# Eight more halves of relation counts made in layer 2 and summed densely in layer 3 of a four-layer graph network

## The chip, the cores and the metric

The kernel runs on one core of one Trainium2 chip. The metric is device time in microseconds (us) for one execution. The core has five engines with queues of their own: PE (TensorE, matrix products), DVE (VectorE), ACT (ScalarE), POOL (GpSimd) and SP (SyncE). Here SP only issues plain DMAs and POOL in the two relational layers only issues gathers, each an indirect DMA that fetches 128 rows of a table.

## The reference, cut to what matters

There are 3125 nodes of 128 features and 100,000 edges, sorted by destination; each edge has one of 8 relations.

```python
# layers 0 and 1: two graph convolutions, then a residual and a layer norm
h   = leaky_relu(gcn_conv(x, src, dst, W1, b1))
x   = layernorm(x + gcn_conv(h, src, dst, W2, b2) * gate + bias)

# layers 2 and 3: two relational layers, then a residual and a layer norm
def rgcn_layer(x, W, SW, b):
    xt  = einsum('nd,rde->rne', x, W)        # a table row for each (relation, node)
    agg = segment_sum(xt[rel, src], dst, 3125)
    return relu(agg + x @ SW + b)
y   = rgcn_layer(rgcn_layer(x, w1, sl1, b1), w2, sl2, b2)
out = layernorm(x + y)
```

## The kernel before, in words

**Two ways to sum over edges.** In the relational layers a destination node gets its sum in one of two ways. *Dense*: the nodes are cut into halves of 32 (`HALF`). For each half a table of counts is made once: for each source node, how many edges it has to each of the 32 nodes by each of the 8 relations (25 source tiles of 128 nodes, 256 columns each, f16, 1.6 MB). Two halves form a pair; the features times the counts of a pair are summed over the 25 source tiles into 512 columns, and two pairs form a quad of 128 nodes, to which the relation weights are applied (`end_quad`, L1484 and L1487). *Sparse*: POOL gathers the table row of each edge, a chunk of 128 edges at a time (L853), and PE multiplies each chunk with a one-hot matrix of destinations (`add_message`, L1462). A chunk serves a window of 64 nodes, and one chunk follows the other at 4 nodes' distance, so that 8 nodes need 2 chunks.

**Who gets which.** `USED, MADE = 40, 48` (L57): layer 2 sums the nodes of 40 halves (1280) densely and gathers for the others; layer 3 sums those of 48 halves (1536) densely. All 48 tables are made in layer 2, beside its sums. Layer 2 has 469 gathers, layer 3 has 405.

**Making the counts.** A half is 8 strips of 4 nodes. For a strip DVE makes four one-hot tiles (`strip_hots`, L1861 twice and L1864 twice), PE multiplies them (`count_rstrip`, L1356, two products of 400 columns, two PSUM banks used by turns), and ACT copies the result into one of four buffers for halves (`turn_counts`, L984). SP stores a full half to memory (L722). 12 strips are counted ahead, beside the tables of layer 2's rows. `Made` works out the order of halves and buffers and deals the strips and the products of layer 2's sums (75 a pair: 25 tiles by 3 bf16 parts, L1427) out to 59 slots, one for each batch of 8 gathers. Two pairs (`STAY`) stay in their buffers and are neither stored nor loaded.

**Layer 3.** It has a slot for each batch of 8 gathers too (51). `spread_sums` deals the tiles of the dense sums out to all slots but the last three: 600 tiles, 25 of them ahead of slot 0, some 12 in a slot. For each tile ACT and DVE by turns widen the f16 counts to fp32 (L1038, L1998, up to 10 tiles ahead, 12 buffers) and PE does two products of 512 columns, with the high and the low part of the features (L1443, L1444). The messages of a slot's batch are set between its tiles. SP loads the counts of a pair (L712, two transfers) as soon as the pair before the previous one has been widened.

**What paces POOL.** In layer 3 POOL issues two gathers of batch n for each quarter of the tiles of slot n-2 that PE has done (a wait on `tile_summed`); in layer 2 the wait is on `rstrip_counted` in the same manner. Six batches of gathered rows have buffers.

```python
if layer == 3 and j % 2 == 0 and n >= AHEAD and sums3[n - AHEAD]:
    steps = steps_until[n - AHEAD + 1] - steps_until[n - AHEAD]
    pool.wait_ge(tile_summed, steps_until[n - AHEAD] + steps * (j // 2 + 1) // 4)
```

**Order on the engines.** Every engine runs a list that is written out ahead, slot by slot, and waits in order. In a slot of layer 2, DVE first copies and splits the tile of layer 3's table whose products PE made one slot earlier (`first_rows` L1985, `low_tile`), then makes the strips' one-hots two strips ahead (three buffers, `HOTS`), with the copy of a finished pair between them (`copy_sums2`, L1969), and then the one-hots of the next slot's batch (L1977). At the end of each node block or quad of layer 3 the result is turned, normalised and stored.

**Keys.** Before all that, with layer 0's counts (`pair_hots`, L1719), each group of 128 strips of two nodes has its relation keys made: the base from destination and source (`make_keys`, L1649), the relation gathered by POOL (L795) and added (`make_rel_keys`, L1670), the keys turned on PE (L1166) and copied by ACT (L900), three groups at a time. 48 halves need 6 groups.

Of the kernel before, what the change touches and what calls it, by code (L numbers as in the profile page):

```python
# [6 lines left out]
P = 128  # L7
# [29 lines left out]
GROUPS = -(-NP // (PAIR * P))  # L37
STRIPS = GROUPS * P
# [15 lines left out]
HSTRIPS = HALF // RSTRIP  # L54
RKEYS = R * TILES
RCELLS = PAIR * RKEYS
USED, MADE = 40, 48  # L57

LAST_BLOCK = 256
RGROUPS = -(-MADE * HALF // (PAIR * P))  # L60
RSTRIPS = RGROUPS * P
PER_CHUNK = 4
BACK, WIN = 32, 64
GATHERS, ONEHOTS, HOTS, RINGS = 6, 4, 3, 4
# [155 lines left out]
def gnn_kernel(nc, x, src, dst, rel, ctx_in, W1, b1, W2, b2, Wg, bg, Wb, w1, sl1, rb1, w2, sl2, rb2, out):  # L220
    f32, i32, f16, bf16 = mybir.dt.float32, mybir.dt.int32, mybir.dt.float16, mybir.dt.bfloat16
    f32r = mybir.dt.float32r
    ALU, ACT, AX = mybir.AluOpType, mybir.ActivationFunctionType, mybir.AxisListType
# [6 lines left out]
    with ExitStack() as stack:  # L230
# [10 lines left out]
        def sem(name):  # L241
# [17 lines left out]
        ident = sb("ident", [P, P])  # L259
# [5 lines left out]
        rel_cols = sb("rel_cols", [P, 2, RSTRIPS])  # L265
# [13 lines left out]
        xT = sb("xT", [P, NP])  # L279
        tin = sb("tin", [P, NP])  # L280
# [3 lines left out]
        dst_rows, src_rows, rel_rows, highs = (  # L284
            m.rearrange("p (g e) -> p g e", e=P) for m in (acc[:, 0:STRIPS], xT[:, 0:STRIPS], xT[:, STRIPS:STRIPS + RSTRIPS],
                                                           acc[:, STRIPS:STRIPS + 6 * P]))
        rel_bases = xT[:, STRIPS + RSTRIPS:STRIPS + 2 * RSTRIPS].rearrange("p (g e) -> p g e", e=P)
        hot_cols = edge_mem[:, 0:STRIPS].bitcast(f16).rearrange("p (a s) -> p a s", a=2)
        spare_rows = acc[:, STRIPS + 6 * P:STRIPS + 12 * P].rearrange("p (g e) -> p g e", e=P)

# [7 lines left out]
        def carve(at, n):  # L298
# [50 lines left out]
        ps = stack.enter_context(nc.psum_tensor("ps", [P, 8, BANK], f32))  # L349
# [11 lines left out]
        keys_ready, rel_keys_ready, keys_turned, cols_copied = (  # L361
            sem(n) for n in ("keys_ready", "rel_keys_ready", "keys_turned", "cols_copied"))
# [148 lines left out]

        key_events = [("strips", g) for g in range(GROUPS)] + [("relations", n) for n in range(RGROUPS // 3)]
        columns_until, n = [], 0
        for kind, g in key_events:
            n += 2 if kind == "strips" and g < RGROUPS else 1
# [369 lines left out]
        def _(act):  # L887
# [3 lines left out]
            def copy_columns(e):  # L891
                kind, n = key_events[e]
                act.wait_ge(keys_turned, e + 1)
                if kind == "strips":
                    keys = ps[:, KEY_BANK, 0:2 * P].rearrange("p (a s) -> p a s", a=2)
                    nc.scalar.activation(hot_cols[:, :, n * P:(n + 1) * P], keys, ACT.Copy).then_inc(cols_copied, 1)
                    if n < RGROUPS:
                        nc.scalar.activation(rel_cols[:, 0, n * P:(n + 1) * P], keys[:, 0, :], ACT.Copy).then_inc(cols_copied, 1)
                else:
                    nc.scalar.activation(rel_cols[:, 1, n * 3 * P:(n + 1) * 3 * P], ps[:, KEY_BANK, 0:3 * P], ACT.Copy).then_inc(cols_copied, 1)  # L900

            def evacuate_units(h):
                b, at = 2 * h // UNIT_BLOCK, 2 * h % UNIT_BLOCK * PAIR * CH
# [242 lines left out]
        def _(pe):  # L1146
# [8 lines left out]
            def turn_keys(e):  # L1155
                kind, n = key_events[e]
                if e:
                    pe.wait_ge(cols_copied, columns_until[e - 1])
                if kind == "strips":
                    pe.wait_ge(keys_ready, 1 + next(i for i, groups in enumerate(PREP_SETS) if n in groups))  # L1160
                    for a, rows in enumerate((src_rows, first_keys if n in PREP_SETS[0] else dst_rows)):
                        last = nc.tensor.transpose(ps[:, KEY_BANK, a * P:(a + 1) * P], rows[:, n, :], ident[:, :])
                else:
                    pe.wait_ge(rel_keys_ready, 1)
                    for a in range(3):
                        last = nc.tensor.transpose(ps[:, KEY_BANK, a * P:(a + 1) * P], rel_rows[:, 3 * n + a, :], ident[:, :])  # L1166
                last.then_inc(keys_turned, 1)

            pe.wait_ge(ident_ready, 1)
# [953 lines left out]
```

## Time and profile before

| | |
|---|---|
| time, median of 3 runs | 1634.54 us (1631.26 to 1634.96) |
| time of the profiled execution | 1633.26 us |
| span of the profiled execution, first to last instruction | 1631.4 us |
| mean granted clock of TensorE, 1 = 2.4 GHz | 0.962 |
| PE busy | 1434.2 us, 88% |
| POOL busy | 928.4 us, 57% |
| DVE busy | 907.0 us, 56% |
| ACT busy | 696.2 us, 43% |
| layer 2's slots, layer 3's slots | about 456 to 1082 us, about 1094 to 1622 us of the span |

Busy PE is not PE at its peak: a matmul's record reaches until its result is complete, and records overlap. What a product costs is the distance between the starts of two that follow each other without a gap. A row of a timeline that merges several instructions gives the start of the first.

### The profile page before, as it was taken

How to read it: one execution, taken by the hardware profiler on the slowest of the kernel's cores; microseconds unless marked ns; L12 is line 12 of the kernel's file. 1: busy time of each engine (PE TensorE's matmuls, PEld its weight loads, DVE VectorE, ACT ScalarE, POOL GpSimd, SP SyncE). 2: the span in 40 equal slices, each digit the busy share in tenths (PEclk: the TensorE clock that was granted, in tenths of full speed). 3: DMA queues.
4: the chain of work that ended last, by engine and by line, in shares of the span. 5: the costliest groups of instructions: out<-in, count | busy, mean ns of one | idle time of the engine just before them, and what ended most of it. 6: DMA issues, size and time to landing. Idle time of an engine off the chain costs nothing.

```text
span 1631.4 us, 24835 instructions
## 1 busy us (share of the span) xinstructions
PE 1434.2 (88%) x9144; PEld 986.7 (60%) x9144; DVE 907.0 (56%) x2665; ACT 696.2 (43%) x1024; POOL 928.4 (57%) x931
## 2 busy tenths in 40 slices
PE   1479989999879999999999999997888978889885
PEld 1364554444436656666666666666767867777775
DVE  8989992134756756657666765643333433334431
ACT  1465541011544645546455554553434444334430
POOL 6700000000067777767777777747777777777775
PEclk9999999999989999999999999998989998899997
DMA  4311340452455545646555554425655665555631
GB/s 135 122 82 82 132 176 37 161 203 101 180 183 173 212 158 199 213 172 215 185 192 209 187 186 177 132 91 213 215 215 214 215 219 199 187 182 214 220 126 48
DMA packets 67474, 275.82 MB, mean 169 GB/s; under 512 B 19988, under 2 KB 25854, under 8 KB 54676
## 3 DMA queue, kind: packets, MB, share of 16 engines
q1 hardware_dynamic: 37940, 213.87, 34.0%
q0 software_dynamic: 29408, 60.29, 13.3%
q8 instruction: 76, 1.25, 0.3%
q14 instruction: 50, 0.41, 0.1%
HBM read 153.70 MB, written 120.38 MB: 168 GB/s over the span
## 4 chain that ended last, share of the span: by engine, by line
PE 68%; DVE 14%; DMA 9%; issue 4%; POOL 4%; ACT 1%; POOLq 0%; DVEq 0%; ACTq 0%
PE ps L1427 20%; PE ps L1462 9%; DVE hot_mem L1719 9%; PE ps L1322 8%; PE ps L1443 8%; PE ps L1356 7%; PE ps L1444 6%; DMA node_id<-table_rel,edges 4%; DMA acc<-table_rel,edges 4%; PE ps L1501 3%; PE ps L1365 2%; POOL node_id L853 2%; PE ps L1487 2%; POOL acc L853 1%; DVE xn L1969 1%
## 5 line engine op out<-in xcount | busy, mean ns | idle before, releaser
L853 POOL DMA_INDIRECT node_id<-table_rel,edges x445 | 442.6, 995 | 499.5 <-DMA table_rel<-node_id 358.3
L853 POOL DMA_INDIRECT acc<-table_rel,edges x429 | 426.1, 993 | 155.0 <-issue 106.1
L1427 PE MATMUL ps<-blocks,raw 128*128 128x512 f16 x1500 | 440.9, 381 | 7.5 <-DVE xn L1969 6.7
L984 ACT ACTIVATE blocks<-ps 128x800 f16<-128x800 f32 x384 | 319.2, 837 | 230.4 <-PE ps L1356 228.7
L1462 PEld LDWEIGHTS ps<-raw,node_id 128*128 128x128 f32 x996 | 191.5, 200 | 113.3 <-issue 60.3
L1861 DVE TENSOR_SCALAR hot_mem<-cell_h,rel_cols 128x128 f16<-128x128 f16 x768 | 167.8, 273 | 160.4 <-PE ps L1356 158.2
L1462 PEld LDWEIGHTS ps<-raw,acc 128*128 128x128 f32 x962 | 179.9, 196 | 85.7 <-issue 37.5
L1864 DVE TENSOR_SCALAR hot_mem<-cell_h,rel_cols 128x400 f16<-128x400 f16 x768 | 226.2, 336 | 0.0
L1427 PEld LDWEIGHTS ps<-blocks,raw 128*128 128x128 bf16 x1500 | 160.1, 113 | 95.1 <-issue 15.0
L1462 PE MATMUL ps<-raw,node_id 128*128 128x64 f32 (+14 forms) x996 | 167.3, 255 | 55.8 <-DMA node_id<-table_rel,edges 55.8
L1356 PE MATMUL ps<-hot_mem 128*128 128x400 f16 x768 | 190.8, 334 | 3.9 <-DVE hot_mem L1864 2.6
L1462 PE MATMUL ps<-raw,acc 128*128 128x64 f32 (+13 forms) x962 | 157.4, 252 | 31.9 <-DMA acc<-table_rel,edges 31.9
L1719 DVE TENSOR_TENSOR hot_mem<-hot_mem,edges 128x2048 f16<-128x2048 f16 x200 | 164.0, 908 | 0.9 <-PE ps L1178 0.6
L1998 DVE CAST conv_hots<-blocks 128x512 fp32r<-128x512 f16 x150 | 65.2, 441 | 174.8 <-PE ps L1444 174.7
L1443 PE MATMUL ps<-conv_hots,high 128*128 128x512 f32 x300 | 147.5, 492 | 1.3 <-ACT conv_hots L1038 1.3
L1038 ACT ACTIVATE conv_hots<-blocks 128x512 fp32r<-128x512 f16 x150 | 92.6, 628 | 124.8 <-PE ps L1444 124.8
L1443 PE MATMUL ps<-conv_raw,high 128*128 128x512 f32 x300 | 138.3, 461 | 0.0
L1038 ACT ACTIVATE conv_raw<-blocks 128x512 fp32r<-128x512 f16 x150 | 93.1, 629 | 68.0 <-PE ps L1444 68.0
L1356 PEld LDWEIGHTS ps<-hot_mem 128*128 128x128 f16 x768 | 76.3, 107 | 74.9 <-issue 30.3
L1998 DVE CAST conv_raw<-blocks 128x512 fp32r<-128x512 f16 x150 | 68.2, 456 | 86.3 <-PE ps L1444 84.5
L1178 PE MATMUL ps<-hot_mem 128*128 128x50 f16 x1600 | 65.1, 195 | 51.4 <-DVE hot_mem L1719 49.9
L909 ACT ACTIVATE blocks<-ps 128x800 f16<-128x800 f32 x100 | 82.9, 837 | 61.5 <-PE ps L1178 61.3
(199 smaller groups left out, 1787.0 us busy)
## 6 DMA issues: line engine op xcount, KB each, us to landing
rcounts<-blocks SPq DMA_DIRECT2D x44, 1600.0 KB, 6.0
blocks<-rcounts SPq DMA_DIRECT2D x44, 1600.0 KB, 7.2
counts<-blocks SPq DMA_DIRECT2D x6, 3200.0 KB, 10.9
blocks<-counts SPq DMA_DIRECT2D x5, 3200.0 KB, 10.4
table_rel<-node_id SPq DMA_DIRECT2D x50, 256.0 KB, 2.1
table_rel<-xn SPq DMA_DIRECT2D x50, 256.0 KB, 2.4
node_id<-table_rel,edges POOLq DMA_INDIRECT x445
acc<-table_rel,edges POOLq DMA_INDIRECT x429
```

Source lines behind the costliest of these rows:

```text
L853: nc.gpsimd.indirect_dma_start(got[m % GATHERS][:, j, :], None, tables_rel[layer - 2], bass.IndirectOffsetOnAxis(ap=row_i[:, first + j:fir ...
L984: nc.scalar.activation(to.rearrange("p t (b m) -> p t b m", b=2), ps[:, strip_bank(k):strip_bank(k) + 2, 0:RCELLS].rearrange("p b (m t) -> ...
L1038: nc.scalar.activation(wide_tile(i).rearrange("p (h n) -> p h n", h=2), narrow_tile(i), ACT.Copy).then_inc(act_wide, 1)
L1322: nc.tensor.matmul(total, part, buffer_of(i)[:, t * n:(t + 1) * n], start=first, stop=False)
L1356: last = nc.tensor.matmul(ps[:, strip_bank(k) + c, 0:RCELLS], rlow_hot[:, k % HOTS, c, :], rcell_hot[:, k % HOTS, c, :], start=True, stop= ...
L1427: last = nc.tensor.matmul(ps[:, SUM_BANK, 0:2 * HCOLS], parts[:, c, t, :], half_pairs[u % 2][:, :, t * HCOLS:(t + 1) * HCOLS], start=(k == ...
L1443: nc.tensor.matmul(ps[:, u % 2, 0:2 * HCOLS], high3(t), wide_tile(i), start=(k == 0), stop=False)
L1462: last = nc.tensor.matmul(ps[:, GATHER_BANK, a - start_:b - start_], got[m % GATHERS][:, j, :], nodehot[:, m % ONEHOTS, j, a - base:b - ba ...
L1719: last = nc.vector.tensor_tensor(hot[:, u, :, :, :], each_h[:, 0:n, :].unsqueeze(1).to_broadcast([P, CH, n, 2]), keys.unsqueeze(2).to_broa ...
L1861: nc.vector.tensor_scalar(rlow_hot[:, u, c, :], cell_h[:, 0:P], rel_cols[:, 0, first + c:first + c + 1], 0.0, ALU.subtract, ALU.is_equal)
L1864: last = nc.vector.tensor_scalar(rcell_hot[:, u, c, :], cell_h[:, :], rel_cols[:, 1, first + c:first + c + 1], 0.0, ALU.subtract, ALU.is_e ...
L1998: nc.vector.tensor_copy(wide_tile(i).rearrange("p (h n) -> p h n", h=2), narrow_tile(i)).then_inc(dve_wide, 1)
```

## The change

56 halves are made in layer 2 in place of 48, and layer 3 sums all 56 (1792 nodes) densely. Layer 2 still uses 40. What follows from the constants: 64 more strips; 28 pairs in layer 3 in place of 24 (700 tiles in place of 600, 14 quads in place of 12); 341 gathers in layer 3 in place of 405, so 43 slots in place of 51, with 17 tiles in a slot in place of 12; 386 messages in place of 450; 52 halves stored and 52 loaded in place of 44 each. Layer 2 keeps its 59 slots and 469 gathers, with 6 to 8 strips in most slots in place of 5 to 8; 41 slots have 8, before 10 did; of the 23 slots in which DVE copies a tile of the table, 17 have 8, before 3 did. Seven groups of relation keys in place of 6 are turned in steps of four and three in place of three and three, and their bases lie in `tin` in place of `xT`, where seven groups would not fit.

```diff
--- before.py
+++ after.py
@@ -54,11 +54,12 @@
 HSTRIPS = HALF // RSTRIP
 RKEYS = R * TILES
 RCELLS = PAIR * RKEYS
-USED, MADE = 40, 48
+USED, MADE = 40, 56
 
 LAST_BLOCK = 256
 RGROUPS = -(-MADE * HALF // (PAIR * P))
 RSTRIPS = RGROUPS * P
+REL_TURNS = [range(a, min(a + 4, RGROUPS)) for a in range(0, RGROUPS, 4)]
 PER_CHUNK = 4
 BACK, WIN = 32, 64
 GATHERS, ONEHOTS, HOTS, RINGS = 6, 4, 3, 4
@@ -284,7 +285,7 @@
         dst_rows, src_rows, rel_rows, highs = (
             m.rearrange("p (g e) -> p g e", e=P) for m in (acc[:, 0:STRIPS], xT[:, 0:STRIPS], xT[:, STRIPS:STRIPS + RSTRIPS],
                                                            acc[:, STRIPS:STRIPS + 6 * P]))
-        rel_bases = xT[:, STRIPS + RSTRIPS:STRIPS + 2 * RSTRIPS].rearrange("p (g e) -> p g e", e=P)
+        rel_bases = tin[:, 0:RSTRIPS].rearrange("p (g e) -> p g e", e=P)
         hot_cols = edge_mem[:, 0:STRIPS].bitcast(f16).rearrange("p (a s) -> p a s", a=2)
         spare_rows = acc[:, STRIPS + 6 * P:STRIPS + 12 * P].rearrange("p (g e) -> p g e", e=P)
 
@@ -511,7 +512,7 @@
 
 
 
-        key_events = [("strips", g) for g in range(GROUPS)] + [("relations", n) for n in range(RGROUPS // 3)]
+        key_events = [("strips", g) for g in range(GROUPS)] + [("relations", n) for n in range(len(REL_TURNS))]
         columns_until, n = [], 0
         for kind, g in key_events:
             n += 2 if kind == "strips" and g < RGROUPS else 1
@@ -897,7 +898,8 @@
                     if n < RGROUPS:
                         nc.scalar.activation(rel_cols[:, 0, n * P:(n + 1) * P], keys[:, 0, :], ACT.Copy).then_inc(cols_copied, 1)
                 else:
-                    nc.scalar.activation(rel_cols[:, 1, n * 3 * P:(n + 1) * 3 * P], ps[:, KEY_BANK, 0:3 * P], ACT.Copy).then_inc(cols_copied, 1)
+                    own = REL_TURNS[n]
+                    nc.scalar.activation(rel_cols[:, 1, own[0] * P:(own[-1] + 1) * P], ps[:, KEY_BANK, 0:len(own) * P], ACT.Copy).then_inc(cols_copied, 1)
 
             def evacuate_units(h):
                 b, at = 2 * h // UNIT_BLOCK, 2 * h % UNIT_BLOCK * PAIR * CH
@@ -1162,8 +1164,8 @@
                         last = nc.tensor.transpose(ps[:, KEY_BANK, a * P:(a + 1) * P], rows[:, n, :], ident[:, :])
                 else:
                     pe.wait_ge(rel_keys_ready, 1)
-                    for a in range(3):
-                        last = nc.tensor.transpose(ps[:, KEY_BANK, a * P:(a + 1) * P], rel_rows[:, 3 * n + a, :], ident[:, :])
+                    for a, g in enumerate(REL_TURNS[n]):
+                        last = nc.tensor.transpose(ps[:, KEY_BANK, a * P:(a + 1) * P], rel_rows[:, g, :], ident[:, :])
                 last.then_inc(keys_turned, 1)
 
             pe.wait_ge(ident_ready, 1)
```

## Rows read from the trace of the kernel before

**Rows 1.** Windows by stage: busy us (instructions) of each engine, granted clock, DMA share, GB/s.

```profile
456.00:1082.00 626.00, 603.74 (x3550) 387.62 (x3551) 398.91 (x1584) 327.80 (x425) 466.94 (x468) 0.99 0.52 181
...
1111.50:1600.80 489.30, 423.75 (x2228) 360.11 (x2229) 174.04 (x423) 198.13 (x330) 374.06 (x379) 0.92 0.55 195
```

**Rows 2.** Waits of PE in layer 2, 456 to 1082: us in total, times, longest.

```profile
PE ps L1462 <- DMA node_id<-table_rel,edges: 7.8, 1, 7.8
PE ps L1427 <- DVE xn L1969: 6.7, 12, 1.2
...
PE ps L1356 <- DVE hot_mem L1864: 1.0, 3, 0.4
```

**Rows 3.** Waits of PE in layer 3, 1111.5 to 1600.8.

```profile
PE ps L1462 <- DMA node_id<-table_rel,edges: 41.2, 11, 6.6
PE ps L1462 <- DMA acc<-table_rel,edges: 26.4, 10, 4.5
```

**Rows 4.** Timeline of PE in a stretch of layer 2: start us, us, what.

```profile
863.26 0.50 PE L1356 MATMUL ps<-hot_mem 128*128 128x400 f16 x2
863.60 0.81 PE L1427 MATMUL ps<-blocks,raw 128*128 128x512 f16 x3
864.25 0.33 PE L1462 MATMUL ps<-raw,node_id 128*128 128x64 f32 x2
864.41 0.59 PE L1427 MATMUL ps<-blocks,raw 128*128 128x512 f16 x2
```

**Rows 5.** Timeline of PE in a stretch of layer 3 without a gap.

```profile
1158.92 0.33 PE L1462 MATMUL ps<-raw,acc 128*128 128x64 f32 x2
...
1160.07 0.33 PE L1462 MATMUL ps<-raw,acc 128*128 128x64 f32 x2
...
1168.10 0.33 PE L1462 MATMUL ps<-raw,acc 128*128 128x64 f32 x2
1168.27 0.44 PE L1484 MATMUL ps<-tin,ws 128*128 128x128 f32 x2
...
1170.25 0.47 PE L1443 MATMUL ps<-conv_hots,high 128*128 128x512 f32 x1
```

**Rows 6.** Window of a stretch of layer 2 in which slots have 8 strips.

```profile
920.00:950.00 30.00, 29.46 (x180) 18.97 (x179) 24.66 (x102) 19.99 (x24) 22.93 (x24) 1.00 0.59 215
```

**Rows 7.** Timeline of DVE in layer 2: copy of a pair, then one-hots, three strips apart.

```profile
548.18 1.03 DVE L1969 COPY xn<-ps 128x512 f32<-128x512 f32 x1 [0.36 <-PE ps L1427]
...
550.52 0.41 DVE L1861 TENSOR_SCALAR hot_mem<-cell_h,rel_cols 128x128 f16<-128x128 f16 x2
...
553.01 0.42 DVE L1861 TENSOR_SCALAR hot_mem<-cell_h,rel_cols 128x128 f16<-128x128 f16 x2
```

**Rows 8.** Chain that ended last: layer 3's first gather, the eighth, its landing.

```profile
1095.79 0.94 POOL acc L853
...
1104.73 6.79 DMA acc<-table_rel,edges
1111.65 0.56 PE ps L1462 x2
...
1278.81 3.62 DMA acc<-table_rel,edges
```

**Rows 9.** Timeline: the first gather after the last tile, the last gather, the last messages.

```profile
1601.91 0.94 POOL L853 DMA_INDIRECT acc<-table_rel,edges  x1 [0.30 <-issue]
...
1618.14 0.94 POOL L853 DMA_INDIRECT node_id<-table_rel,edges  x1 [0.30 <-issue]
...
1621.41 2.37 PE L1462 MATMUL ps<-raw,node_id 128*128 128x64 f32 x10 [3.81 <-DMA node_id<-table_rel,edges]
```

**Rows 10.** Loads of halves in layer 3: us from issue to landing.

```profile
DMA to landing us min/median/max: 6.8/7.2/8.8
```

**Rows 11.** DMA share of the stretch in which a pair was loaded, 1123 to 1133.

```profile
1123.00:1133.00 10.00, 5.92 (x33) 4.83 (x31) 3.19 (x7) 4.00 (x6) 7.56 (x9) 0.89 0.93 374
```

**Rows 12.** Relation keys of six groups: duration min/median/max.

```profile
L1670 DVE SCALAR_TENSOR_TENSOR xT<-xT x1: 954/954/954, 89.9 to 89.9; 128x768 f32<-128x768 int32 x1
```

## The prediction

> **What bounds the kernel now.** I read the busy times by stage first, then PE's waits in the two relational layers, then stretches of the timeline for the price of each product. In layer 2 PE is busy 603.7 of 626 us at a granted clock of 0.99, while POOL is busy 467 [rows 1]; PE waits there once for a gather, 7.8 us at the start, and else in small change [rows 2]. Layer 2 is PE's. In layer 3 PE is busy 423.8 of 489.3 us at 0.92 [rows 1], and it waits for gathered rows 21 times, 67.6 us in all [rows 3]. POOL starts 405 gathers between 1095.79 and 1618.14, the first and the last start: 1.29 us each [rows 8, 9]. Started without a gate they lie 1.25 us apart, as in the stretch after the last tile: 13 steps in 16.2 us [rows 9]. 405 x 1.25 = 506 of these 522 us, so layer 3 is POOL's, and PE's waits are what it has left over. The change takes gathers from POOL in layer 3 and gives PE work in both layers. So the question is what PE needs in each.
>
> **Keys.** One group more: the relation keys on DVE take 0.95 us for six groups [rows 12], so 0.16 more; the base, a transpose, a copy and one more relation gather (POOL is idle there afterwards) are of the same size or hidden. Moving the bases to `tin` costs nothing: `tin` is first written by `scale_x`, four pairs later on the same engine. I take 0.5 us, between 0 and 2.
>
> **Layer 2: 64 more strips.** A strip's two products take 0.34 us on PE (863.26 to 863.60), a product of the dense sum 0.22 and a message 0.16 [rows 4]. PE is the bound, so all of 64 x 0.34 = 21.8 us lies on the path. Beside it: ACT has 64 more copies on an engine busy 328 of 626 us [rows 1], hidden. DVE's one-hots take 0.83 us a strip when nothing gates them (550.52 to 553.01, three strips) [rows 7], so 53 us more on 399 [rows 1], or 452 of some 649: hidden on average. But DVE works in order, 41 slots now have 8 strips and 17 of these also a table tile to copy; a copy of a pair, 1.03 us [rows 7], stands ahead of one-hots, which are made only two strips ahead. In the stretch of such slots that the trace has, DVE was busy 24.7 of 30 us and PE 29.5 [rows 6], and waits of PE for one-hots come to 1.0 us in all of layer 2 [rows 2]. I take 1 us, and 0 to 20 as bounds (half a microsecond in each of 41 slots). SP's 8 more stores of 1.6 MB: a load of that size lands in 7.2 us [rows 10], the DMA engines' share in layer 2 is 0.52 [rows 1], and a buffer comes back only after the next half's 8 strips: hidden; without that cover a store would cost its 7 us. Gathers in layer 2 stay 469; they are paced by strips, and a slot grows from 10.6 to 11 us against POOL's 10.0, so POOL gets slack. Layer 2: +22.8 us.
>
> In the same stretch POOL issued 24 gathers in 30 us, 1.25 us apart, beside a DVE busy for 82% [rows 6]. The Trainium skill, "SBUF — State Buffer", section "Who interferes with whom", says that a DVE operation in a two-port mode, which these one-hots and the casts of layer 3 can be, locks GpSimd out for its whole length, so that descriptors of POOL's DMAs can't be written. By that rule the 53 us of new one-hots would be POOL's loss. The trace does not agree: at 82% of DVE a pace of 1.25 us could not stand.
>
> **Layer 3 on POOL.** 64 gathers fewer: 341 x 1.25 = 426 us, 80 less.
>
> **Layer 3 on PE.** In the stretch without a gap, 1158.92 to 1160.07 holds two tiles and one message (1.15 us), and 1158.92 to 1168.10 holds 15 tiles and 10 messages (9.18 us) [rows 5]. So a tile costs 0.464 and a message 0.222 us, and a quad 1.98 (1168.27 to 1170.25). Counted from the first message at 1111.65 [rows 8], when 27 tiles are done, to the last tile (21 messages and one quad lie behind it):
> - before: 573 tiles 265.9, 429 messages 95.2, 11 quads 21.8, block starts and turns some 7.5 (allowance): 390.4 us, against 489 measured, ending at 1600.8;
> - after: 673 tiles 312.3, 365 messages 81.0, 13 quads 25.7, 7.5: 426.5 us.
>
> A slot of 17 tiles and 8 messages is 9.7 us, 10.4 on average with quads and block starts; POOL's slot is 10.0. So PE becomes the bound, by little. Will it run gapless? The last two gathers of batch n are released by the end of slot n-2, take 2.5 us to issue and 6.8 to land [rows 8], 9.3 us; PE needs them after slot n-1 and three tiles, 10.4 + 1.4 = 11.8 later. 2.5 us are left. That is the order of layer 2 (10.6 against 10.0 and the same gates), where PE's idle time, without the first wait, is 14.5 of 626 us, 2.3% [rows 1, 2]. I take 10 us for this, and 3 for half-clock time and for slots 0 to 3, where POOL's batches land just as PE comes. The last tile then ends at 1111.65 + 426.5 + 13 = 1551.2: 49.6 us earlier.
>
> **The end.** After the last tile 14 gathers were left (1601.91 to 1618.14), then the landing, ten products and the last norm, 30.6 us in all [rows 9]. If PE sets the pace, 7 are left, those released by the last tile and the last batch of 5, or 8.8 us less; if POOL lags, nothing is won. I take 6.6.
>
> **Loads.** A pair of halves takes about 11 us to land (7.2 each, overlapping) [rows 10], at a DMA share of 0.93 [rows 11]. It is sent for when the pair before the previous one is widened and is needed 25 tiles later: 21.7 us before, 25/17 x 10.4 = 15.3 after. 4 us are left, and 10 widened tiles beyond that. Hidden. But gathers landed in 3.6 us where no load ran and in 6.8 beside one [rows 8]; now a load runs 7 us in 10, so the late landing becomes the rule. I have priced it so.
>
> **The sum.** 0.5 + 22.8 - 49.6 - 6.6 = -32.9 us. The profiled execution took 1633.3 us (span 1631.4), so 1600.4; the median of the runs shown is 1.3 above it: 1602 us. Its own range: 1588 (no allowance in layer 3, 8.8 at the end) to 1612 (twice the allowances). A measurement of this kernel can tell some 0.3% (5 us) from no change.
>
> **Rivals.**
> - *A third of the stalls stays.* Layer 3 loses 489 - 390 = 99 us to waits and half clock, 2.06 us a slot. If a third of it stays in 40 slots: 27 us in place of 13, and the end gains 3.6 less. 1620. For it: PE's and POOL's slots differ by only 0.4 us, and the clock falls with each wait of some 3 us.
> - *Half of it stays*: 41 us, the end gains 2 in place of 6.6: 1634, no change.
> - *Lock step, slower.* The gates and the landing, not POOL's number of gathers, make the stalls, and all 2.06 us a slot stay: 82 in place of 13, nothing gained at the end: 1602 + 69 + 7 = 1678. It decides when a landing takes over 9.3 us from issue (6.8 + 2.5), since each slot then ends late and releases its gathers late. Against it: layer 2 has the same gates, nearly the same slot, and hardly a wait [rows 2].
> - *DVE bounds layer 2.* Half a microsecond in 41 slots: 1621. Against it: [rows 6].
> - *The port.* Were POOL's 1.25 us partly DVE's lock, the 53 us would lengthen layer 2 in place of 22: 1633. The pace beside a busy DVE speaks against it [rows 6].
>
> **Chances.** Forecast 0.66; a third of the stalls 0.14; DVE 0.06; half the stalls 0.05; lock step 0.07; port 0.02. Faster by over 0.3%: 0.66 + 0.14 + 0.06 = 0.86. Same: 0.05 + 0.02 = 0.07. Slower: 0.07. The range reaches from 1588 to the third of the stalls and DVE's case with 3 us on top, 1624, and leaves out the rest.
>
> **What the profile would show.** Layer 2 some 23 us longer with PE busy as before and waits on one-hots under 3 us; 448 strips. Layer 3's last tile 50 us earlier on its own clock, that is near 1574; PE's waits for gathers under 20 us there, in place of 67.6; the granted clock at 0.97 or more; gathers 1.3 to 1.35 us apart, now with POOL waiting for tiles; and 7 or 8 gathers behind the last tile. A clock still near 0.92 and a wait in every second slot would show the stalls kept; a wait of the casts for loads would show that loads are not hidden; PE waits on L1864 of 10 us or more would show DVE's case.

## The result and the profile after

| | before | after |
|---|---|---|
| median of the runs, us | 1633.79 (4 runs) | 1579.34 (1579.26 to 1579.51, 4 runs) |
| ratio, 95% interval | | 0.967 (0.965 to 0.968) |
| span of the profiled execution, us | 1631.4 | 1577.7 |
| mean granted clock | 0.962 | 0.988 |
| PE's first to last product of layer 2's sums, us | 623.9 | 640.3 |
| start of the first to start of the last tile of layer 3, us | 506.8 | 444.6 |
| start of the last tile to the end of the span, us | 30.9 | 22.7 |

54 us faster. The forecast was faster by 32 and a range down to 1588: the direction held, the size did not. Two lines are added, one near the top and one at L901, so that line numbers of after are one higher up to there and two higher behind: L1429 is L1427 of before, L1358 is L1356, L1445 and L1446 are L1443 and L1444, L1464 is L1462, L854 is L853, L2000 is L1998.

The page of the changed kernel, its busy line and the clock in 40 slices:

```profile
PE 1452.0 (92%) x9381; PEld 999.4 (63%) x9381; DVE 978.1 (62%) x2967; ACT 785.2 (50%) x1147; POOL 866.8 (55%) x868
...
PEclk9999999999989999999999999999999999999998
```

The windows by stage, as in [rows 1], here cut where the changed kernel's stages lie (busy us and instructions of each engine, granted clock, DMA share, GB/s). The second begins at the first message of layer 3, the third after the last tile:

```profile
456.00:1099.00 643.00, 623.82 (x3681) 399.34 (x3681) 451.67 (x1843) 381.48 (x490) 468.54 (x468) 0.99 0.56 197
...
1128.40:1555.60 427.20, 425.89 (x2337) 365.43 (x2338) 191.28 (x464) 233.43 (x387) 317.78 (x322) 0.99 0.67 245
1555.60:1577.70 22.10, 9.23 (x67) 8.32 (x65) 5.46 (x19) 2.56 (x6) 7.64 (x8) 0.71 0.15 40
```

In layer 3 PE is busy 425.9 of 427.2 us, where before it was busy 423.8 of 489.3. So it now bounds layer 3, with only one gap, of 1.0 us, after the first message. The waits of PE (engine, line, whom it waited for: us in total, times, longest), first in layer 2, where they answer to [rows 2]:

```profile
PE ps L1429 <- DVE xn L1971: 8.6, 16, 1.2
PE ps L1464 <- DMA node_id<-table_rel,edges: 7.5, 1, 7.5
...
PE ps L1358 <- DVE hot_mem L1866: 0.6, 2, 0.3
```

Layer 2 of before had one wait more for a gather, which neither [rows 2] nor the prediction shows. It ends at 573.1 us; in the changed kernel only the wait at the start (7.5 us) is left:

```profile
PE ps L1462 <- DMA acc<-table_rel,edges: 2.3, 1, 2.3
```

In layer 3 of the changed kernel, from the first message to the last tile, the waits answer to [rows 3]:

```profile
PE ps L1464 <- DMA acc<-table_rel,edges: 4.6, 1, 4.6
PE ps L1457 <- ACT tin L1063: 1.0, 1, 1.0
```

21 waits for gathered rows of 67.6 us together have become one of 4.6 us, the one at the first message. POOL's gathers of layer 3 (duration in ns, first and last start, and what POOL's idle time before them ended on):

```profile
L854 POOL DMA_INDIRECT acc<-table_rel,edges x173: 938/944/1360, 1112.5 to 1564.4; - x173
L854 POOL DMA_INDIRECT node_id<-table_rel,edges x168: 940/944/2639, 1123.1 to 1533.9; - x168
...
  PE ps L1446: 43.0, 103
```

341 gathers in 451.9 us are 1.33 us each, and 43.0 us of POOL's idle time end on a tile of PE (L1446), that is on the gates, in place of 24.7 us before (81 times, on L1444). The loads of halves, which the prediction hid, took to landing:

```profile
DMA to landing us min/median/max: 6.9/7.2/8.2
```

### The profile page after: what moved, and what is told of

It is laid out like the page before. It is cut to its first block, busy times and chain, and to the rows that moved or that the text cites. A ratio compares the mean times of both kernels' runs of the same rounds, so it can differ in the third digit from the quotient of the medians.

```text
span 1577.7 us, 25737 instructions
## 1 busy us (share of the span) xinstructions
PE 1452.0 (92%) x9381; PEld 999.4 (63%) x9381; DVE 978.1 (62%) x2967; ACT 785.2 (50%) x1147; POOL 866.8 (55%) x868
## 4 chain that ended last, share of the span: by engine, by line
PE 79%; DVE 15%; issue 2%; POOL 2%; DMA 1%; ACT 1%; POOLq 0%; DVEq 0%; ACTq 0%
PE ps L1429 20%; PE ps L1445 11%; PE ps L1446 10%; PE ps L1464 9%; DVE hot_mem L1721 9%; PE ps L1358 9%; PE ps L1324 8%; PE ps L1503 3%; PE ps L1489 3%; PE ps L1367 3%; DVE xn L1971 1%; DMA acc<-table_rel,edges 1%; POOL acc L854 1%; POOL acc L796 1%; POOL node_id L854 0%
## 5 line engine op out<-in xcount | busy, mean ns | idle before, releaser
L854 POOL DMA_INDIRECT node_id<-table_rel,edges x408 | 409.6, 1004 | 502.1 <-DMA table_rel<-node_id 358.7
L854 POOL DMA_INDIRECT acc<-table_rel,edges x402 | 397.9, 990 | 160.1 <-issue 92.4
L986 ACT ACTIVATE blocks<-ps 128x800 f16<-128x800 f32 x448 | 372.6, 836 | 209.7 <-PE ps L1358 204.9
L1429 PE MATMUL ps<-blocks,raw 128*128 128x512 f16 x1500 | 440.7, 380 | 8.6 <-DVE xn L1971 8.6
L1863 DVE TENSOR_SCALAR hot_mem<-cell_h,rel_cols 128x128 f16<-128x128 f16 x896 | 193.7, 272 | 132.9 <-PE ps L1358 127.8
L1866 DVE TENSOR_SCALAR hot_mem<-cell_h,rel_cols 128x400 f16<-128x400 f16 x896 | 260.4, 332 | 0.0
L1358 PE MATMUL ps<-hot_mem 128*128 128x400 f16 x896 | 222.5, 333 | 3.6 <-DVE hot_mem L1866 2.3
L1429 PEld LDWEIGHTS ps<-blocks,raw 128*128 128x128 bf16 x1500 | 157.6, 111 | 102.7 <-issue 16.3
L1464 PEld LDWEIGHTS ps<-raw,node_id 128*128 128x128 f32 x906 | 169.2, 190 | 55.6 <-issue 9.1
L1464 PEld LDWEIGHTS ps<-raw,acc 128*128 128x128 f32 x924 | 168.7, 192 | 56.2 <-issue 13.2
L1464 PE MATMUL ps<-raw,acc 128*128 128x64 f32 (+10 forms) x924 | 146.6, 247 | 10.7 <-DMA acc<-table_rel,edges 10.7
L1445 PE MATMUL ps<-conv_hots,high 128*128 128x512 f32 x352 | 154.0, 438 | 1.3 <-ACT conv_hots L1040 1.3
L1464 PE MATMUL ps<-raw,node_id 128*128 128x64 f32 (+10 forms) x906 | 146.3, 244 | 7.5 <-DMA node_id<-table_rel,edges 7.5
L1445 PE MATMUL ps<-conv_raw,high 128*128 128x512 f32 x348 | 152.4, 438 | 0.1
L1358 PEld LDWEIGHTS ps<-hot_mem 128*128 128x128 f16 x896 | 89.3, 109 | 80.1 <-issue 31.2
L1040 ACT ACTIVATE conv_hots<-blocks 128x512 fp32r<-128x512 f16 x176 | 108.2, 630 | 60.4 <-PE ps L1446 60.1
L2000 DVE CAST conv_hots<-blocks 128x512 fp32r<-128x512 f16 x176 | 78.8, 458 | 87.7 <-PE ps L1446 86.7
L2000 DVE CAST conv_raw<-blocks 128x512 fp32r<-128x512 f16 x174 | 76.4, 449 | 81.7 <-PE ps L1446 80.7
L911 ACT ACTIVATE blocks<-ps 128x800 f16<-128x800 f32 x100 | 82.8, 838 | 61.2 <-PE ps L1180 61.0
```

The lines of the kernel that those rows point to most:

```text
L854: nc.gpsimd.indirect_dma_start(got[m % GATHERS][:, j, :], None, tables_rel[layer - 2], bass.IndirectOffsetOnAxis(ap=row_i[:, first + j:fir ...
L986: nc.scalar.activation(to.rearrange("p t (b m) -> p t b m", b=2), ps[:, strip_bank(k):strip_bank(k) + 2, 0:RCELLS].rearrange("p b (m t) -> ...
L1040: nc.scalar.activation(wide_tile(i).rearrange("p (h n) -> p h n", h=2), narrow_tile(i), ACT.Copy).then_inc(act_wide, 1)
L1358: last = nc.tensor.matmul(ps[:, strip_bank(k) + c, 0:RCELLS], rlow_hot[:, k % HOTS, c, :], rcell_hot[:, k % HOTS, c, :], start=True, stop= ...
L1429: last = nc.tensor.matmul(ps[:, SUM_BANK, 0:2 * HCOLS], parts[:, c, t, :], half_pairs[u % 2][:, :, t * HCOLS:(t + 1) * HCOLS], start=(k == ...
L1445: nc.tensor.matmul(ps[:, u % 2, 0:2 * HCOLS], high3(t), wide_tile(i), start=(k == 0), stop=False)
```

## The experiments

Each kernel was timed in turns with the kernel before on the same chip; the ratio is to that, with its 95% interval.

**The keys alone.** All of the changed code, with the old number of halves.

```diff
-USED, MADE = 40, 56
+USED, MADE = 40, 48
```

> 48 halves as before, with the new code for the relation keys: turned in steps of four and two groups in place of three and three, bases in the other memory. My theory (the whole change lies in the two relational layers): 1634 us, within 3. Rival (the keys' part carries some of the 54 us gained, or costs some): 5 us or more away from 1634.

1634.6 us, ratio 1.000 (0.999 to 1.002). The turning of the keys in other steps and their other memory cost nothing and bring nothing that can be measured. This kernel has six groups of keys, not seven; the seventh is made before layer 2, whose first product of sums starts at 456.6 us in the changed kernel and at 456.3 before, so it costs nothing that shows either.

**52 and 60 halves.**

```diff
-USED, MADE = 40, 56
+USED, MADE = 40, 52
```

> 52 halves made and dense in layer 3. My theory (layer 3 lasts as long as the longer of POOL's and PE's work): POOL needs 373 x 1.25 = 466 us there, PE some 409, so layer 3 is still POOL's. At before's 1.29 us a gather it is 32 x 1.29 = 41 us shorter than before, layer 2 is 32 x 0.34 = 11 us longer less up to 5 for a wait that goes away: 1599 to 1604 us, with PE waiting for gathers 20 us or more in layer 3. Rival (gain in proportion to the halves, no change of bound): half way, 1607 us.

1603.5 us, ratio 0.981 (0.979 to 0.983), within what was expected. Waits of PE in its layer 3:

```profile
PE ps L1464 <- DMA acc<-table_rel,edges: 22.9, 8, 4.5
PE ps L1464 <- DMA node_id<-table_rel,edges: 11.5, 5, 3.8
```

13 waits for gathers, 34.4 us (4.5 of them at the first message): at 52 halves layer 3 is still POOL's. The time is also only 3.5 us from the rival's 1607; it is the waits that decide between the two.

```diff
-USED, MADE = 40, 56
+USED, MADE = 40, 60
...
-        stats = sb("stats", [P, TILES, 6])
+        stats = sb_over("stats", [P, TILES, 6], f32, "wgate")
```

> 60 halves made and dense in layer 3. My theory (at 56 halves PE already bounds layer 3): 50 tiles more x 0.464 = 23, 32 messages fewer x 0.222 = 7, a quad 2, and 32 strips x 0.34 = 11 in layer 2: 29 us more than the changed kernel, 1608 us. Rival (POOL's gathers still bound at 56 halves, and 27 us go with every 4 halves): 1552 us.

1601.1 us, ratio 0.980 (0.978 to 0.982): 22 us slower than at 56, and not 29. The direction and the bound are as expected. The window of its layer 3:

```profile
1138.00:1577.00 439.00, 437.87 (x2354) 373.90 (x2354) 195.90 (x484) 251.03 (x414) 280.55 (x290) 1.00 0.68 249
```

And the waits of PE in its layer 2:

```profile
PE ps L1464 <- DMA node_id<-table_rel,edges: 6.4, 1, 6.4
PE ps L1429 <- DVE xn L1971: 5.3, 11, 0.5
```

PE is busy 437.9 of 439 us of layer 3, as good as gapless again. My sum for it was too high for reasons that can be read off: 60 halves leave three node blocks for the gathers in place of four, so one edge between blocks less, where 15 chunks are multiplied twice (47 messages fewer than at 56 halves, not 32; 3.3 us), and in layer 2 the waits for the copy of a pair (L1429 behind DVE) shrank from 8.6 to 5.3 us; and in layer 3 the mean clock is 1.00 in place of 0.99. 56 is the lowest of the three.

**The halves made, but not used.** 56 halves in layer 2; layer 3 sums 48 and gathers for the rest. The numbers of the halves are exchanged so that the two that stay in their buffers are 46 and 47.

```diff
-USED, MADE = 40, 56
+USED, MADE, DENSE3 = 40, 56, 48
...
-        gathers = {2: Gathers(USED * HALF), 3: Gathers(MADE * HALF)}
+        gathers = {2: Gathers(USED * HALF), 3: Gathers(DENSE3 * HALF)}
...
-        STEPS3 = TILES * (MADE // 2)
+        STEPS3 = TILES * (DENSE3 // 2)
```

> 56 halves are made in layer 2, but layer 3 sums 48 densely and gathers for the rest as before; the result is whole. My theory: layer 2 grows by the 16.7 us seen in the changed kernel (21.8 for 64 strips, less 5 for the wait for a gather at 577 us that goes away in longer slots): 1651 us. Rival (strips are cheaper than 0.34 us and the wait at 577 has nothing to do with it): that wait is seen again. Rival (the number of halves in layer 2 is paid again in layer 3's loads or end): over 1656 us.

1649.5 us, ratio 1.010 (1.008 to 1.012), 16.1 above the kernel before beside it. Layer 2's part is 16 to 17 us, as in the changed kernel, and not the 22.8 of my sum. Why it is less shows in one stretch, 570 to 600 us. Before, with 48 halves:

```profile
570.00:600.00 30.00, 27.06 (x154) 17.28 (x153) 17.40 (x69) 13.87 (x18) 22.69 (x25) 0.94 0.44 146
```

The same stretch with the keys alone (48 halves):

```profile
570.00:600.00 30.00, 27.07 (x156) 17.42 (x155) 17.57 (x68) 13.78 (x19) 22.70 (x24) 0.94 0.47 162
```

With layer 3 alone (48 halves, below):

```profile
570.00:600.00 30.00, 27.06 (x155) 17.30 (x153) 17.31 (x69) 13.74 (x19) 22.69 (x25) 0.94 0.45 146
```

With 52 halves:

```profile
570.00:600.00 30.00, 29.34 (x178) 19.10 (x177) 20.42 (x82) 16.32 (x21) 22.69 (x25) 1.00 0.50 172
```

The changed kernel, with 56:

```profile
570.00:600.00 30.00, 29.62 (x182) 19.26 (x180) 21.02 (x84) 17.25 (x22) 22.69 (x24) 1.00 0.56 195
```

And 56 halves made but not used:

```profile
570.00:600.00 30.00, 29.63 (x180) 19.25 (x179) 20.06 (x81) 17.13 (x23) 22.68 (x25) 1.00 0.59 213
```

With 48 halves PE is busy 27.1 of 30 us at a clock of 0.94, in all three kernels; with 52 or more 29.3 to 29.6 at 1.00. POOL starts 24 or 25 gathers in each: it runs at its full pace of 1.25 us in all six. With 48 halves most slots up to there have 5 or 6 strips and PE needs less than POOL's 10 us for one, so it catches up with POOL and waits for a gather, from 570.8 to 573.1; with 8 strips in most of them it does not. With 52 halves the slots are longer only in part, and two short waits (1.0 and 1.3 us) end at 626 and 637 us instead. The 64 strips cost the 64 x 0.34 = 21.8 us of the sum: PE is busy 623.8 us in place of 603.7 [rows 1], 20.1 more, and 0.06 of 30 us of clock, or 1.8, are no longer in that. What comes back is these 1.8 and idle time: 22.3 us before and 643.0 - 623.8 = 19.2 after, 3.1 less. 2.3 of this is the wait for the gather. The other 0.8 is what is left of small changes both ways: the waits for the copy of a pair grew from 6.7 to 8.6 us, others fell by some 2.7.

**Layer 3 alone.** 48 halves made, layer 3 sums 28 pairs; the four pairs more are loaded from other nodes' counts.

```diff
-USED, MADE = 40, 56
+USED, MADE, DENSE3 = 40, 48, 56
...
-PAIR_ORDER3 = [*STAY, *(w - 1 for w in STAY)]
+STAY3 = (DENSE3 // 2 - 1, USED // 2 - 1)
+PAIR_ORDER3 = [*STAY3, *(w - 1 for w in STAY3)]
...
-rcounts_dram[2 * PAIR_ORDER3[p] + h, :, :]
+rcounts_dram[2 * {23: 0, 24: 1, 25: 2, 26: 3}.get(PAIR_ORDER3[p], PAIR_ORDER3[p]) + h, :, :]
```

> 48 halves are made as before, layer 3 sums 56 densely; the counts of the eight more halves (nodes 1472 to 1791) are those of other nodes, loaded from memory a second time. My theory (the layers' shares add up): 62 us less between layer 3's first and last tile and 8 less behind it, as in the changed kernel, with layer 2 as before: 1563 us. Rival (layer 3's gain needs the longer layer 2, say by POOL or DMA work that is over by then): 1570 us or more.

1561.9 us, ratio 0.955 (0.953 to 0.957). The kernel before beside it took 1636.9, so 75.0 less; against the 1633.8 of before elsewhere, 71.9. The layers' parts add up to within 1.3 to 4.4 us: +16.1 and -72 to -75 against -54.5 of both.

**Fewer gathers, no more tiles.** The kernel before, with layer 3's gathers from node 1792 on.

```diff
-        gathers = {2: Gathers(USED * HALF), 3: Gathers(MADE * HALF)}
+        gathers = {2: Gathers(USED * HALF), 3: Gathers(56 * HALF)}
```

> The kernel before (48 halves) with layer 3's gathers from node 1792 on in place of 1536: the messages of nodes 1536 to 1791 are left out in layer 3, and their output. My theory (layer 3 of before is POOL's work alone): 64 gathers fewer at 1.29 us, 82 us less, 1551 us, that is more than the 71 us that layer 3 gave in the changed kernel, where PE became the bound; PE still waits for gathers, since it has 600 tiles only. Rival (layer 3's time comes from PE's and POOL's waits for each other, whatever the number of gathers per slot): the same 10.0 us a slot as before, but 2.06 us a slot of waits and half-clock time stay and PE's share is unchanged: less than 71 us are won.

That run, and the two of the end in the same batch (below), fell on a chip on which the kernel before took 1853 us (1826 to 1874), and ACT and DVE waited up to 11 us at a time for something that the profile puts outside the core; 1758.3 us, ratio 0.955 (0.947 to 0.964), tells nothing about some microseconds. So it was run again:

> Again the kernel before with layer 3's gathers from node 1792 on in place of 1536 (the messages of nodes 1536 to 1791, and their output, left out), since the times of its first run and of the kernel before beside it scattered by over 2%. My theory, as before: 64 x 1.29 = 82 us less, 1551 us, more than the 71 us of the changed kernel's layer 3. Rival: less than 71 us.

1557.9 us, ratio 0.952 (0.950 to 0.955), 76.2 less than the kernel before beside it. POOL's gathers in its layer 3:

```profile
L853 POOL DMA_INDIRECT acc<-table_rel,edges x173: 939/947/1360, 1099.3 to 1544.4; - x173
L853 POOL DMA_INDIRECT node_id<-table_rel,edges x168: 941/946/3128, 1109.9 to 1517.4; - x168
```

And PE's waits from the first message to the last tile:

```profile
PE ps L1462 <- DMA node_id<-table_rel,edges: 19.5, 8, 3.4
PE ps L1462 <- DMA acc<-table_rel,edges: 10.5, 6, 4.5
```

341 gathers from 1099.3 to 1544.4 are 1.31 us each, near the 1.29 of before, and PE, with only 600 tiles, still waits 14 times. So fewer gathers shorten layer 3, and by more than the changed kernel's 71, though by 6 to 7 us less than the 82 expected. The messages of these 64 gathers are left out with them, but they are only 64 x 0.222 = 14 us of PE's work and could not give 76. That before's layer 3 was bound by its gathers, and not by PE's products, is shown.

**One PSUM bank for layer 3's sums,** as layer 2 has it.

```diff
-                        if u >= 2:
-                            pe.wait_ge(half_copied, PAIRS2 + u - 1)
+                        if u:
+                            pe.wait_ge(half_copied, PAIRS2 + u)
...
-                    nc.tensor.matmul(ps[:, u % 2, 0:2 * HCOLS], high3(t), wide_tile(i), start=(k == 0), stop=False)
+                    nc.tensor.matmul(ps[:, 0, 0:2 * HCOLS], high3(t), wide_tile(i), start=(k == 0), stop=False)
```

> The changed kernel with layer 3's sums in one PSUM bank in place of two by turns, as layer 2 has it: the next pair's first product waits until ACT has copied the last one's sum. My theory (PE's small change of waits in layer 2 comes from that one bank and from a late gather, and layer 3 has neither, so it runs gapless): the copy takes 1.1 us and a semaphore each way, 27 times some 1.4 us, 38 us more: 1617 us. Rival (the wait is filled by work already queued): 1580 us.

1622.1 us (1615.1 to 1627.5), ratio 0.991 (0.987 to 0.994), 43 us above the changed kernel; the profile is of a run of 1626.8. Its waits in layer 3:

```profile
PE ps L1445 <- ACT raw L1048: 30.4, 26, 3.3
PE ps L1464 <- DMA acc<-table_rel,edges: 3.9, 2, 3.1
```

26 waits for ACT's copy of a pair's sum, 30.4 us. Layer 2 has this wait in small (8.6 us in 16 waits, above), layer 3 with its two banks has none.

**POOL's gates later.**

```diff
-pool.wait_ge(tile_summed, steps_until[n - AHEAD] + steps * (j // 2 + 1) // 4)
+pool.wait_ge(tile_summed, min(steps_until[n - AHEAD] + steps * (j // 2 + 1) // 4 + 8, STEPS3))
```

> The changed kernel with POOL's gates in layer 3 eight tiles (nearly half a slot, 4.6 us) later. My theory (a batch's last gathers are 9.3 us from release to landing and have 2.5 us to spare): first message to first message becomes 3 us of tiles to the release and 9.3 for the gather, 12.3 us in place of 10.4, some 38 times: 72 us and some half-clock time on top, 1650 to 1675 us. Rival (POOL runs far enough ahead, so the gates have much more than 2.5 us to spare): 1579 to 1590 us.

1620.1 us (1616.1 to 1626.4), ratio 0.991 (0.987 to 0.994). 41 us slower than the changed kernel, so the gates have only a few microseconds to spare; but not the 72 expected, so it is more than my 2.5. PE's waits for gathers in its layer 3:

```profile
PE ps L1464 <- DMA node_id<-table_rel,edges: 14.5, 11, 2.7
PE ps L1464 <- DMA acc<-table_rel,edges: 14.4, 7, 4.5
```

These are 18 waits, 28.9 us, and 4.5 of it is the wait at the first message, which the changed kernel has too (4.6). So 17 of 40 slots have a new wait, 24.4 us together: a gate 4.6 us later costs 0.6 us a slot. That puts the spare time at 4.0 us or more in the mean over the slots, an estimate from this one shift; in the slots that wait it was less than 4.6, in the others more. The rest of the 41 us is mostly time at half clock (mean clock 0.980 in place of 0.988, some 13 us), and a longer end. I had priced every landing at 6.8 us; some land sooner, as the one in 3.62 us [rows 8].

**36 halves used in layer 2.** An attempt to shorten layer 2, where PE is the bound in the changed kernel.

```diff
-USED, MADE = 40, 56
+USED, MADE = 36, 56
```

> 56 halves made, but 36 in place of 40 summed densely in layer 2, 32 gathers more there. PE has 150 products x 0.217 less and 32 messages x 0.16 more: 27 us less. POOL has 501 gathers x 1.25 = 626 us in place of 586, against a layer 2 of 643. My theory (each layer lasts as long as the longer of the two): layer 2 becomes POOL's, 626 and some waits: 1565 to 1580 us. Rival (POOL never bounds layer 2): 1552 us. Rival (waits and half clock as in layer 3 of before): 1590 us or more.

1589.0 us, ratio 0.971 (0.970 to 0.973): 10 us slower than the changed kernel, out of my range and nearest to the last of the three cases (1590 us or more). POOL's gathers of its layer 2:

```profile
L854 POOL DMA_INDIRECT node_id<-table_rel,edges x259: 941/947/1772, 456.2 to 1104.1; - x130
L854 POOL DMA_INDIRECT acc<-table_rel,edges x240: 940/947/1700, 487.7 to 1080.3; - x120
```

And PE's waits there:

```profile
PE ps L1464 <- DMA acc<-table_rel,edges: 17.5, 9, 6.1
PE ps L1464 <- DMA node_id<-table_rel,edges: 10.4, 4, 8.0
```

499 of the 501 gathers, from 456.2 to 1104.1, are 1.30 us each, and PE waits 13 times, 27.9 us. So this layer 2 runs at about the 1.29 of before's layer 3, not at the 1.25 that I had taken here.

**The end.** Layer 3's tiles dealt out to all slots but the last two, or but the last one, in place of three.

```diff
-        a, b = (n + n * (pairs - 1) * min(t, slots - 3) // (slots - 3) for t in (s, s + 1))
+        a, b = (n + n * (pairs - 1) * min(t, slots - 2) // (slots - 2) for t in (s, s + 1))
```

> The changed kernel with layer 3's tiles dealt out to all slots but the last two in place of the last three. My theory (behind the last tile the path is POOL's: gathers released by it or unissued, 1.25 us each, a landing, ten products and the last norm): the last batch of 5 is released before the last tile, so 5 gathers fewer, some 6 us, and 8 messages move ahead of it: 1573 us, within 2. Rival (the end is PE's or the norms' work): 1579 us.

> The changed kernel with layer 3's tiles dealt out to all slots but the last one. My theory: all gathers are issued before the last tile's slot ends, but the last quad and its norm now stand behind the last tile and the last messages: 1570 to 1574 us. Rival (the last quad's chain costs more than the gathers saved): 1576 us or more.

Both fell on the chip that scattered: 1782.3 and 1790.5 us, ratios 0.966 (0.958 to 0.975) and 0.971 (0.962 to 0.981), inconclusive. The first was run again with the changed kernel beside it:

> Again the changed kernel with layer 3's tiles dealt out to all slots but the last two, for the same reason. My theory: 5 gathers fewer behind the last tile, 6 us: 1573 us, within 2. Rival (the end is PE's or the norms' work): 1579 us.

> The changed kernel once more, beside the two others on one chip, as the base for the few microseconds at the end: 1579 us, within 2.

1577.5 us (1577.4 to 1578.9, five runs), ratio 0.965 (0.964 to 0.967), and 1580.1 us (1579.5 to 1581.9, five runs), ratio 0.967 (0.965 to 0.969). The first is 2.6 us faster; the runs of the two do not overlap. It is the fastest whole kernel of this study, but by less than half of what was expected. Windows of its end, up to its last tile and behind it:

```profile
1556.00:1563.30 7.30, 7.30 (x40) 6.18 (x39) 1.86 (x6) 0.63 (x1) 5.47 (x7) 1.00 0.21 56
1563.30:1577.00 13.70, 5.78 (x50) 5.35 (x48) 3.32 (x13) 2.37 (x5) 0.56 (x1) 0.86 0.10 26
```

13.7 us are left behind the last tile in place of some 22, but the tile itself ends 7 us later than in the changed kernel beside it (1563.3 against 1556.5). Some 3 us of this are messages that stood behind it and now stand ahead. The rest is mostly waits: PE's waits from the first message to the last tile are these,

```profile
PE ps L1464 <- DMA acc<-table_rel,edges: 5.1, 2, 4.2
PE ps L1464 <- DMA node_id<-table_rel,edges: 2.3, 2, 1.5
```

and beside the one at the first message (4.2 us) they hold three of 3.2 us together, where the changed kernel has none. That is about the 3.4 us by which the gain fell short of the 6 expected. The same tiles in one slot more are fewer in a slot (16.5 in place of 16.9 in the mean), which brings PE nearer to POOL; that this is why the waits are back is argued, not tested.

## Why the prediction was wrong

**Right.** What bounds which layer, and that the bound moves from POOL to PE. The sum of PE's products in layer 3, within 1%: 426.5 us worked out from two stretches of the timeline [rows 5], 426.6 measured from the first message (1128.6) to the last product of the last tile (1555.2), the point that was 1600.8 before. That the two agree to 0.1 us is luck. The measured time also holds a gap of 1.0 us and a stretch at half clock right behind the first message, which costs some 3 us:

```profile
1128.40:1134.70 6.30, 6.08 (x18) 5.09 (x19) 1.01 (x3) 1.26 (x2) 4.78 (x6) 0.51 0.23 57
1134.70:1555.60 420.90, 419.81 (x2321) 360.34 (x2320) 190.27 (x462) 232.17 (x385) 313.00 (x317) 1.00 0.68 248
```

So the products themselves took about 422.5, and the sum, with its 7.5 us of allowance for block starts, was 4 too high. The price of a strip, 0.34 us, and DVE and ACT beside it: DVE is busy 451.7 of 643 us and PE waits 0.6 us for one-hots. The loads stayed hidden (7.2 us again). The keys cost nothing that can be measured; I had taken 0.5. One reading was loose: the landing of 3.62 us [rows 8], put down as one "where no load ran", fell into the end of a load, at a DMA share of 0.69 against 0.95 for the landing of 6.79.

**The step that failed: the allowance in layer 3.** "I take 10 us for this, and 3 for half-clock time" is what the prediction set on the 426.5, with the 2.3% of idle time that layer 2 has beside its first wait. The last tile came 426.6 us after the first message and not 439.5: 12.9 of the 21 us of error lie here. The 3 us for half clock came. Of the 10 only a gap of 1.0 us came, which is 9 us of error; the other 4 are the sum that was too high. Layer 2's idle time was read as what two engines of nearly equal pace cost each other. Most of it is something else, in the trace of before already. Of its 14.5 us, 6.7 are waits for the copy of a pair [rows 2], which come with the one bank of layer 2's sums; 2.6 stand ahead of a quad's products (L1484) with no wait that the profile shows; and only 2.3, the wait that ends at 573.1 us, are for a gather. Layer 3 has two banks, and with one bank it lost 43 us. And here PE, 0.4 us a slot slower than POOL, had no wait for it behind the first message: six batches have buffers, and the spare time is nearer to 4 us than to the 2.5 that I had counted.

**The step mis-sized in layer 2.** "All of 64 x 0.34 = 21.8 us lies on the path", and 1 more for DVE and 0.5 for the keys: 23.3, measured 16.4 to 17 (16.7 at the first tile of layer 3, 1110.4 against 1093.7). The products are the right price. What the sum lacked is that longer slots also take away a wait of before: the gathers that bounded layer 3 bounded layer 2 for a moment too, up to 573.1 us. "PE waits there once for a gather" was a misreading: there were two such waits, the second of 2.3 us with a stretch at half clock behind it, and they make 4.1 of the some 5 us that came back. The windows of six kernels with 40 halves used show it, by the number of halves made alone. The first message came at 1128.6 and not at 1111.65 + 23.3: 6.3 us of the error.

**The end.** 6.6 us were taken, 8.1 came (22.5 from 1555.2 to the end of the span, in place of 30.6). In the trace of the changed kernel (start, duration), the last gathers after the last tile, and the last messages:

```profile
1555.22 0.39 PE L1446 MATMUL ps<-conv_hots,low 128*128 128x512 f32 x1
1555.22 0.42 PEld L1464 LDWEIGHTS ps<-raw,node_id 128*128 128x128 f32 x2
1555.32 0.95 POOL L854 DMA_INDIRECT acc<-table_rel,edges  x1 [0.30 <-issue]
...
1564.43 0.94 POOL L854 DMA_INDIRECT acc<-table_rel,edges  x1 [0.30 <-issue]
...
1567.79 2.36 PE L1464 MATMUL ps<-raw,acc 128*128 128x64 f32 x10 [5.15 <-DMA acc<-table_rel,edges]
```

8 gathers start after 1555.22, in place of 14: 7.5 us less, where I had counted 7 and 8.8. Of the 2.2 us that I had held back for a POOL that lags, 1.5 were not needed.

12.9, 6.3 and 1.5 are 20.7 us, which is the error: the span expected was 1598.5, the measured one 1577.7.

**The rivals.** A third or half of the stalls, or all of them, did not stay: one wait of 4.6 us and a granted clock of 0.99 in layer 3 against 0.92. Waits on the gates are a real danger here, though: with the gates 4.6 us later 24 us of waits are back and the kernel takes 41 us more, though not the 72 expected there. DVE did not bound layer 2. The port: POOL's gathers in layer 2 keep their duration, with a median of 945 ns (944 and 945 before), while DVE's work there grew from 399 to 452 us:

```profile
L854 POOL DMA_INDIRECT node_id<-table_rel,edges x240: 938/945/1681, 454.4 to 1072.5; - x120
L854 POOL DMA_INDIRECT acc<-table_rel,edges x229: 938/945/1807, 485.7 to 1095.2; - x115
```

So the rule of the Trainium skill ("SBUF — State Buffer", "Who interferes with whom") that a two-port operation of DVE stops GpSimd's descriptors does not show in these one-hots. No run here shows in which mode they ran.

**The range.** Its low end, 1588 (1602 less 13 and less 2.2 is 1587), left out the allowances of layer 3 but held layer 2's 22.8 fixed, with no lower bound beside 0 to 20 more. A change of slots that takes a wait away is a gain that the rows allowed: PE's 22.3 us of idle time in layer 2 [rows 1] were the room for it. With layer 2 as long as predicted the kernel would have taken 1579.3 + 6.3 = 1585.6 us, still a little below that end, by the sum of products that was 4 too high.

## What to carry to other kernels

Where one engine feeds another, price the next bound as the plain sum of its own instructions, each from a stretch without a gap; add idle time only with a cause that the new order also has, not as a percentage of a neighbouring stage. Before adding it, ask of every wait of the old trace whether the change also removes it, in the stages that are only made longer too. In this kernel a layer that the feeding engine bounded ran 3 to 5% over that engine's unhindered pace (1.29 to 1.31 against 1.25 us a gather, three times), and one that the fed engine bounded ran within 1% of its sum. Of the three splits tried the best is the one in which the fed engine is just the slower one. The margin is thin: with the same tiles dealt out to one slot more, 3 us of waits were back.

## What was not expected of the hardware

With one bank for layer 3's sums, the granted clock was once at half for 17 us (1521.9 to 1539.0) though no wait of PE just before it was long. Three windows of that kernel:

```profile
1500.00:1530.00 30.00, 26.96 (x132) 22.89 (x132) 10.56 (x25) 13.74 (x23) 17.14 (x18) 0.87 0.62 234
1530.00:1550.00 20.00, 18.87 (x87) 16.06 (x86) 7.17 (x24) 7.28 (x13) 9.62 (x9) 0.78 0.47 169
1550.00:1570.00 20.00, 18.59 (x105) 15.80 (x104) 8.61 (x22) 9.97 (x17) 13.13 (x15) 1.00 0.67 242
```

From 1530 to 1550 PE is busy 18.9 of 20 us and the mean clock is 0.78; just before the fall it had two waits, of 1.04 and 1.03 us, that end at 1520.0 and 1522.3. From 1550 to 1570 it is busy 18.6 of 20 us at 1.00. Both levels (1.2 and 2.4 GHz) were so granted at nearly the same busy share, though a busy PE does less at the lower one (87 matmuls against 105). Single waits of about 1 us, some 16 us apart, stand all along this layer and left the clock at full elsewhere. It need not happen: of the six runs of this kernel three took 1627 us at a mean clock of 0.980 and three 1615 to 1618 us at 0.986 to 0.988. That this stretch is the whole difference is not shown, since the profile is of one of the three of 1627 us and none was taken of the others. In the changed kernel layer 3 ran at full clock but for the stretch behind the first message.

Whether a gather lands in 3 or 7 us seems to go with the loads beside it (3.62 us at a DMA share of 0.69, 6.79 at 0.95 [rows 8]), but this was not tried by itself, and the spare time of the gates is known only from the one shift by eight tiles.
